# Turning the experts' input by transposing DMAs from block 2 on, with actor and router as fp16 passes over its halves

## The chip, the cores and the metric

The kernel runs on one core of a Trainium2 chip. The metric is device time in microseconds (us) of one execution; the median of the runs shown stands for a kernel.

## The reference, cut to what matters

64 batches of 128 tokens with 128 features. Each token is normalised, attends to the 120 context tokens of its batch (queries, keys and values from `Wq`, `Wk`, `Wv`), and the result is added. Then comes a mixture of experts over the normalised sum `h`:

```
probs  = softmax(h @ router_w.T)                       # 8 experts
a_h    = gelu(h @ actor_w1.T + actor_b1)               # 50 units
k      = argmax(clip(a_h @ actor_w2.T + actor_b2)) + 1 # 1 to 6
scores = where(rank(probs) < k, probs, 0)
out    = sum over e of scores[e] * ((silu(h @ gate[e].T) * (h @ up[e].T)) @ down[e].T)
result = x + out
```

All eight experts are computed for every token; a score of zero drops one. Each expert has 336 hidden units.

## The kernel before, in words

A block is four batches, so 512 tokens, and there are 16 blocks. The 8 x 336 hidden units are cut into 21 tiles of 128 rows (16 units of each expert). For a tile and a block there are three products of 128 x 128 by 128 x 512: `gate`, `up` and `down`. Each is made from fp16 halves in three passes, weights high by input low, weights low by input high, high by high (`split_product`, L408 to L412), so a tile costs TensorE nine fp16 matmuls of 512 columns. The weights are scaled by powers of two, found in the first turn, and cut into halves there (`weight_tops`, `weight_top`, `weight_scales`, `weight_low`).

Each engine runs its own program in an order written out by hand. A turn `t` has 21 steps `j`. In step `j` TensorE does the gate of tile `j + 2`, the up of tile `j` and the down of tile `j - 3` of block `t`. Between these, at a fixed `j`, each engine does a piece of the other work: the attention of block `t + 2`, and the second normalisation's turning, actor, router and ranking of block `t + 1`. ScalarE makes the silu of a tile (`gated`) and the high half of the hidden values (`high`), GpSimd weighs the silu with the scores (`weigh`), VectorE multiplies it by `up` (`hidden`) and makes the low half (`low`). Semaphores tie the engines together. Turns 0 to 3 and 12 to 16 are written out, turns 4 to 11 are a loop on the chip.

The experts' input of block `t + 1` is made as follows. ScalarE normalises it at the end of the turn before (`norm2`, tokens by partition). TensorE turns it at `j = 1` by four fp32 transposes (`turn_x2`, L362), ScalarE copies it from PSUM (`turned_x2`, L581) and casts the high half (`x2_high`, L586), GpSimd makes the low half (`x2_low`, L794). At `j = 3` `actor_router` (L369) multiplies the turned fp32 input by 64 columns of actor and router weights, twice: even 128-token groups into partitions 0 to 63, odd ones into 64 to 127. `actor`, `square` (ScalarE), `actor_arg` (VectorE), `tanh` (ScalarE), `actor_gelu` (VectorE) and `logits` (TensorE, `j = 8`) follow.

The scores of a block, spread over the 128 rows of a tile as two fp16 halves, are turned by two transposing DMAs (`turn_scores`, L278) at the end of the turn. They, the loads of x and ctx and the stores are all issued by the sync engine, in program order. `stats_1`, `aggregate_1` (VectorE) and `rstd_1` (GpSimd) begin the first normalisation of block `t + 3` from x; `turn_x` (L312), `turned_x` and `energies` (L324) carry on that of block `t + 2`.

Of the kernel before, what the change touches and what calls it, by code (L numbers as in the profile page):

```python
# [8 lines left out]
F16 = mybir.dt.float16  # L9
# [5 lines left out]
P = 128  # L15
# [37 lines left out]
W_TOP = (2.0 ** 8, 2.0 ** 15, 2.0 ** 15)  # L53
# [14 lines left out]
def program(nc, x, ctx_t, consts, consts16, gate_t, up_t, down_t, out):  # L68
# [4 lines left out]
    with ExitStack() as stack:  # L73
# [42 lines left out]
        w_max = sb("w_max", [P, 3])  # L116
        w_top_col, w_one, w_top = sb("w_top_col", [2, 2]), sb("w_one", [2, P]), sb("w_top", [2, 2 * P])
        w_half = sb("w_half", [P, 3])
        w_pow = sb("w_pow", [P, 3])
        w_inv = sb("w_inv", [P, 3])  # L120
        w_mul = sb("w_mul", [P, 3])
# [24 lines left out]
        xn_lo = [sb(f"xn_lo{k}", [P, NT], F16) for k in range(2)]  # L146

# [52 lines left out]
        hi_ready, lo_ready = sem("hi_ready"), sem("lo_ready")  # L200
        ah_done, a_ready, sq_ready, arg_ready, tanh_ready, gelu_ready, al_done, al_ready = (
# [29 lines left out]
        def upto(n):  # L231

            return min(n + 1, BLOCKS) if isinstance(n, int) else n + 1

# [15 lines left out]
        @block.sync  # L250
        def _(sp):
            def load_x(n, par):
                wait(sp, x2_ready, n - 1)
                sp.dma_start(x_in[par][:], x_blocks[n]).then_inc(x_loaded[par], 16)

            def load_ctx(n, par):
                wait(sp, vp_done, n - 1)
                sp.dma_start(ctx_in[par][:], ctx_blocks[n]).then_inc(ctx_loaded[par], 16)

            def load_weights(k, w):  # L260
                for c in range(3):
                    cols = slice(c * PART * P, (c + 1) * PART * P)
                    sp.dma_start(raw[k][:, cols], w[:, cols]).then_inc(weights_in[3 * k + c], 16)

            load_x(0, 0)
            load_ctx(0, 0)
            load_x(1, 1)
            load_ctx(1, 1)
            load_weights(0, gate_t)
            load_weights(1, up_t)  # L270
            load_weights(2, down_t)
            for n in range(2, 4):
                load_ctx(n, n % 2)
                load_x(n, n % 2)

            def turn_scores(n):
                for dst, src in ((unit_hi, spread_hi), (unit_lo, spread_lo)):
                    sp.dma_start(dst[:].rearrange("p (b n) -> p b n", b=BB), src[:], transpose=True)\  # L278
                        .then_inc(units_in, 16)

            def turn(t, par):
                if is_block(t + 4):
                    load_ctx(t + 4, par)
                if is_block(t + 1):
                    sp.wait_ge(spread_lo_ready, t + 1)
                if is_block(t + 4):
                    sp.dma_start(x_in[par][:], x_blocks[t + 4]).then_inc(x_loaded[par], 16)  # L290
                if is_block(t + 1):
                    turn_scores(t + 1)
                if is_block(t - 1):
                    sp.wait_ge(out_ready, t)
                    sp.dma_start(out_blocks[t - 1], out_sb[1 - par][:]).then_inc(stored[1 - par], 16)

            turns(sp, turn)
            for par in range(2):
                sp.wait_ge(stored[par], 16 * (BLOCKS // 2))

        @block.tensor
        def _(pe):
# [69 lines left out]

            def probs_transposes(n, dst=x1):
                pe.wait_ge(exp_done, n + 1)
                if dst is x1:
                    wait(pe, al_ready, upto(n - 1))
                if isinstance(n, int) and n < 2:
                    pe.wait_ge(kt_ready, n + 1)
                for b in range(BB):
                    last = transpose(dst[0:CTX, b * P:(b + 1) * P], probs[:, b, :], ident_sb)  # L380
                last.then_inc(pt_done, 1)
# [45 lines left out]
            def gate(t, par, j):  # L427
                n = TILES * t + j
                if isinstance(t, int) and t == 0 and j == 0:
                    pe.wait_ge(w_mul_ready, 1)  # L430
                if j == 0:
                    pe.wait_ge(hi_ready, t + 1)
                    pe.wait_ge(lo_ready, t + 1)
                if isinstance(t, int) and t == 0 and j % PART == 0:
# [29 lines left out]
            def turn(t, par):  # L464
                nxt = 1 - par
                for j in range(TILES):
                    if isinstance(t, int) and t == 0 and j == 2:
                        weights_turned(1, 2, 3)
                    if isinstance(t, int) and t == 0 and j == 4:
                        weights_spread(1, 2, 3)  # L470
# [68 lines left out]
        def _(act):  # L539
# [23 lines left out]
            def norm2(n, lo, hi):  # L563
                act.wait_ge(ln2_shift, n + 1)
                wait(act, t2_done, n)
# [21 lines left out]

            def keys(n, src=x1):
                act.wait_ge(kp_done, n + 1)
                wait(act, e_done, n)  # L590
                af(k_t[:], src[:, 0:NC], ACT.Identity, bias=key_col[:]).then_inc(kt_ready, 1)

            def actor(n):
                act.wait_ge(ah_done, n + 1)
                wait(act, gelu_ready, n)
                af(a_sb[:], x1[:, 0:2 * P], ACT.Identity, bias=b1_col).then_inc(a_ready, 1)

            def square(n):
                act.wait_ge(a_ready, n + 1)
                af(x1[:, 0:2 * P], x1[:, 0:2 * P], ACT.Square, bias=b1_root[:], scale=sq_scale[:]).then_inc(sq_ready, 1)  # L600
# [59 lines left out]
            def turn(t, par):  # L660
                nxt = 1 - par
                for j in range(TILES):
# [12 lines left out]
                    if j == 1 and is_block(t + 1):  # L675
                        turned_x2(t + 1)
                    if j == 2 and is_block(t + 1):
                        x2_high(t + 1, nxt)
                    if j == 4 and is_block(t + 1):
                        actor(t + 1)  # L680
                        square(t + 1)
# [23 lines left out]
                    if j == 20 and is_block(t + 2):  # L705
                        norm2(t + 2, 2, BB)
                    if isinstance(t, int) and t == 0 and j == 0:
                        keys(2)
# [12 lines left out]
            act.wait_ge(setup_pool, 8)  # L721
# [32 lines left out]
        def _(pool):  # L754
# [7 lines left out]
            for k in range(3):  # L762
                g.memset(w_half[:, k:k + 1], W_TOP[k] / 2).then_inc(setup_pool, 1)
            pool.wait_ge(setup_pool, 8)
# [93 lines left out]
            def turn(t, par):  # L858
                nxt = 1 - par
                for j in range(TILES):  # L860
# [5 lines left out]
                    if j == 2 and is_block(t + 3):  # L866
                        rstd_1(t + 3)
                    if j == 3 and is_block(t + 1):
# [3 lines left out]
                    if j == 11 and is_block(t + 1):  # L872
                        count_less(t + 1)
# [26 lines left out]
        def _(dve):  # L900
# [8 lines left out]
            def weight_tops(i, lo, hi):  # L909
                dve.wait_ge(w_stat, 3)  # L910
                dve.wait_ge(w_sum_ready, 3 * i + 3)
                v.tensor_reduce(w_max[:, lo:hi], w_abs[:, lo:hi, :], AX.X, ALU.max).then_inc(w_max_ready, 1)
# [9 lines left out]
            def weight_scales(i, lo, hi):  # L922
# [9 lines left out]
                if i == 0:  # L932
                    dve.wait_ge(setup_pool, 8)
# [195 lines left out]
            def turn(t, par):  # L1129
                nxt = 1 - par  # L1130
                for j in range(TILES):
                    if j == 0 and is_block(t + 3):
                        stats_1(t + 3, nxt)
                    if j == 5 and is_block(t + 1):
# [31 lines left out]
                    if isinstance(t, int) and t == 0 and j == 3:  # L1166
                        weight_top(1, 2, 3)
                    if isinstance(t, int) and t == 0 and j == 5:
                        weight_scales(1, 2, 3)
                        result_scale()  # L1170
                    if isinstance(t, int) and t == 0 and j in LOW_AT:
# [3 lines left out]
                    if j == 1 and is_block(t + 3):  # L1175
# [10 lines left out]
                    if j == 1 and is_block(t + 3):  # L1186
# [22 lines left out]
            v.memset(w_one[:], 1.0)  # L1209
            norm1(0, 0)  # L1210
# [107 lines left out]
```

## Time and profile before

| | us |
|---|---|
| median of 3 runs (801.4 to 803.35) | 802.43 |
| the profiled execution | 804.05 |
| its span, first to last instruction | 802.2 |

The profile is of one execution. Busy time of TensorE overlaps itself, because matmuls are pipelined and their ends are modelled: what a matmul costs the stream is the distance from its start to the next one's. Lines such as L362 are those of the kernel before.

### The profile page before, as it was taken

How to read it: one execution, taken by the hardware profiler on the slowest of the kernel's cores; microseconds unless marked ns; L12 is line 12 of the kernel's file. 1: busy time of each engine (PE TensorE's matmuls, PEld its weight loads, DVE VectorE, ACT ScalarE, POOL GpSimd, SP SyncE). 2: the span in 40 equal slices, each digit the busy share in tenths (PEclk: the TensorE clock that was granted, in tenths of full speed). 3: DMA queues.
4: the chain of work that ended last, by engine and by line, in shares of the span. 5: the costliest groups of instructions: out<-in, count | busy, mean ns of one | idle time of the engine just before them, and what ended most of it. 6: DMA issues, size and time to landing. Idle time of an engine off the chain costs nothing.

```text
span 802.2 us, 13994 instructions
## 1 busy us (share of the span) xinstructions
PE 773.1 (96%) x3848; PEld 391.4 (49%) x3848; DVE 627.1 (78%) x1351; ACT 591.0 (74%) x1032; POOL 553.8 (69%) x621
## 2 busy tenths in 40 slices
PE   7578999999999999999999999999999999999997
PEld 4333455454545545454554545555454555544443
DVE  4898878787787868868786887878688786877775
ACT  3577777877786777777777777777778778677654
POOL 2375776868587685858768586776858677686763
PEclk9699999999999999999999999999999999999999
DMA  7100101001010010101001010100101000010100
GB/s 293 40 1 13 27 2 32 21 13 40 14 40 2 14 40 13 39 12 39 0 12 39 12 39 12 39 0 12 39 12 41 0 23 6 1 27 0 28 1 27
DMA packets 37151, 21.41 MB, mean 27 GB/s; under 512 B 17264, under 2 KB 35824, under 8 KB 37104
## 3 DMA queue, kind: packets, MB, share of 16 engines
q1 hardware_dynamic: 36816, 20.39, 9.0%
q10 hardware_dynamic: 288, 0.48, 0.2%
q8 instruction: 19, 0.31, 0.2%
q14 instruction: 28, 0.23, 0.1%
HBM read 12.73 MB, written 4.19 MB: 21 GB/s over the span
## 4 chain that ended last, share of the span: by engine, by line
PE 91%; DVE 4%; issue 2%; POOL 1%; ACT 1%; DMA 1%; DVEq 0%; POOLq 0%; ACTq 0%
PE bank L410 26%; PE bank L412 26%; PE bank L411 26%; PE bank L341 2%; PE bank L406 2%; PE bank L333 2%; PE bank L324 2%; PE bank L369 1%; PE bank L395 1%; PE bank L362 1%; PE bank L312 1%; DVE bank L1120 1%; PE bank L380 1%; PE bank L386 1%; DVE hid_lo L1126 1%
## 5 line engine op out<-in xcount | busy, mean ns | idle before, releaser
L855 POOL TENSOR_TENSOR weighted<-silu,score_bc 128x512 f32<-128x512 f32 x336 | 427.0, 1277 | 183.6 <-ACT silu L657 175.6
L1120 DVE SCALAR_TENSOR_TENSOR bank<-bank,h_scale,weighted 128x512 f32<-128x512 f32 x336 | 253.1, 753 | 133.8 <-PE bank L412 110.1
L651 ACT ACTIVATE hid_hi<-bank 128x512 f16<-128x512 f32 x336 | 200.4, 596 | 155.4 <-DVE bank L1120 154.3
L657 ACT ACTIVATE silu<-bank,silu_scale 128x512 f32<-128x512 f32 x336 | 230.4, 686 | 27.7 <-PE bank L412 26.5
L1126 DVE TENSOR_TENSOR hid_lo<-bank,hid_hi 128x512 f16<-128x512 f32 x336 | 228.1, 679 | 10.7 <-ACT hid_hi L651 10.6
L410 PE MATMUL bank<-xn_lo,gate_hi 128*128 128x512 f16 x336 | 128.0, 381 | 4.9 <-DVE gate_lo L947 4.9
L410 PE MATMUL bank<-hid_lo,down_hi 128*128 128x512 f16 x336 | 127.9, 381 | 0.6 <-DVE hid_lo L1126 0.6
L410 PE MATMUL bank<-xn_lo,up_hi 128*128 128x512 f16 x336 | 127.4, 379 | 0.8 <-DVE hid_lo L1126 0.7
L411 PE MATMUL bank<-hid_hi,down_lo 128*128 128x512 f16 x336 | 127.9, 381 | 0.0
L412 PE MATMUL bank<-hid_hi,down_hi 128*128 128x512 f16 x336 | 127.9, 381 | 0.0
L412 PE MATMUL bank<-xn_hi,gate_hi 128*128 128x512 f16 x336 | 127.8, 380 | 0.0
L411 PE MATMUL bank<-xn_hi,gate_lo 128*128 128x512 f16 x336 | 127.8, 380 | 0.0
L412 PE MATMUL bank<-xn_hi,up_hi 128*128 128x512 f16 x336 | 127.6, 380 | 0.0
L411 PE MATMUL bank<-xn_hi,up_lo 128*128 128x512 f16 x336 | 127.6, 380 | 0.0
L410 PEld LDWEIGHTS bank<-xn_lo,up_hi 128*128 128x128 f16 x336 | 32.8, 98 | 41.7 <-DVE hid_lo L1126 2.3
L410 PEld LDWEIGHTS bank<-hid_lo,down_hi 128*128 128x128 f16 x336 | 33.0, 98 | 41.3 <-DVE hid_lo L1126 1.8
L412 PEld LDWEIGHTS bank<-hid_hi,down_hi 128*128 128x128 f16 x336 | 33.0, 98 | 39.9 <-issue 0.6
L412 PEld LDWEIGHTS bank<-xn_hi,gate_hi 128*128 128x128 f16 x336 | 32.9, 98 | 40.0 <-issue 0.5
L411 PEld LDWEIGHTS bank<-hid_hi,down_lo 128*128 128x128 f16 x336 | 33.0, 98 | 39.7 <-issue 0.6
L410 PEld LDWEIGHTS bank<-xn_lo,gate_hi 128*128 128x128 f16 x336 | 34.4, 102 | 36.8 <-issue 11.7
L412 PEld LDWEIGHTS bank<-xn_hi,up_hi 128*128 128x128 f16 x336 | 32.9, 98 | 39.6
L411 PEld LDWEIGHTS bank<-xn_hi,up_lo 128*128 128x128 f16 x336 | 32.9, 98 | 39.2
(145 smaller groups left out, 840.1 us busy)
## 6 DMA issues: line engine op xcount, KB each, us to landing
x_in<-in_x SPq DMA_DIRECT2D x16, 256.0 KB, 2.7
out<-out_sb SPq DMA_DIRECT2D x16, 256.0 KB, 2.3
ctx_in<-in_ctx_t SPq DMA_DIRECT2D x16, 240.0 KB, 2.6
raw_gate<-in_gate_t SPq DMA_DIRECT2D x3, 448.0 KB, 6.3
raw_up<-in_up_t SPq DMA_DIRECT2D x3, 448.0 KB, 8.1
raw_down<-in_down_t SPq DMA_DIRECT2D x3, 448.0 KB, 9.8
consts_sb<-in_consts ACTq DMA_DIRECT2D x1, 403.0 KB, 3.6
unit_hi<-spread_hi SPq DMA_TRANSPOSE x15, 3.0
```

Of the source, the lines that this page charges most:

```text
L324: last = mm(dst[:, b * CTX:(b + 1) * CTX], xn_t[:, b * P:(b + 1) * P], k_t[:, b * CTX:(b + 1) * CTX], start=True, stop=True)
L333: last = mm(dst[0:CTX, b * P:(b + 1) * P], ctx_in[par][:, b * CTX:(b + 1) * CTX], wv_t, start=True, stop=True)
L341: last = mm(dst[:, b * P:(b + 1) * P], probs_t[:, b * P:(b + 1) * P], v_sb[:, b * P:(b + 1) * P], start=True, stop=True)
L406: mm(dst[:, 0:NC], key_t[:], ctx_in[par][:], start=True, stop=True).then_inc(kp_done, 1)
L410: mm(dst, w_hi[w][:, cols], lo, start=start, stop=False)
L411: mm(dst, w_lo[w][:, cols], hi, start=False, stop=False)
L412: return mm(dst, w_hi[w][:, cols], hi, start=False, stop=stop)
L651: af(hid_hi[j % HRING][:], up_bank[j % U_BANKS][:], ACT.Copy).then_inc(hid_hi_ready, 1)
L657: af(silu[j % RING][:], gate_bank[(par + j) % G_BANKS][:], ACT.Silu, scale=silu_scale[:])\
L855: g.tensor_tensor(weighted[j % RING][:], silu[j % RING][:], score_bc[par][:], ALU.mult)\
L1120: v.scalar_tensor_tensor(up_bank[j % U_BANKS][:], up_bank[j % U_BANKS][:], h_scale[:], weighted[j % RING][:], ALU.mult, ALU.mult).then_inc ...
L1126: v.tensor_tensor(hid_lo[j % HRING][:], up_bank[j % U_BANKS][:], hid_hi[j % HRING][:], ALU.subtract)\
```

## The change

For blocks 0 and 1 (`by_tensor`) the input is turned as before, except that the actor and router products stand at `j = 5`. For blocks 2 to 15 ScalarE casts the high half from the unturned input at `j = 0` (`token_high`), GpSimd makes the low half at `j = 1` (`token_low`), and two transposing DMAs write the turned halves into `xn_hi` and `xn_lo`. `turn_x2`, `turned_x2` and the old casts go for these blocks. Actor and router become six fp16 matmuls of 256 columns at `j = 5` over halves of weights and input; their weights get a power-of-two scale, found in the first turn beside that of `down`, and `actor` and `square` undo it.

The sync engine's order in a turn becomes: wait for the high half, store block `t - 2`, turn the high half, wait for the low half, load x of block `t + 3`, turn the low half, wait for the spread scores, load ctx of block `t + 4`, turn the two halves of the scores. The statistics of x move from `j = 0` and `1` to `4` and `5`, `rstd_1` from `2` to `6`, `actor` and `square` from `4` to `5`, `actor_arg` from `5` to `6`.

```diff
+        xn2_hi, xn2_lo = sb("xn2_hi", [P, NT], F16), sb("xn2_lo", [P, NT], F16)
+        ar_hi, ar_lo = sb("ar_hi", [P, HALF], F16), sb("ar_lo", [P, HALF], F16)
...
+        def by_tensor(n):
+            return isinstance(n, int) and n < 2
...
+            def turned(dst, src):
+                return sp.dma_start(dst[:].rearrange("p (b n) -> p b n", b=BB), src[:], transpose=True)
             def turn(t, par):
-                if is_block(t + 4):
-                    load_ctx(t + 4, par)
+                by_dma = is_block(t + 1) and not by_tensor(t + 1)
+                if by_dma:
+                    sp.wait_ge(hi_ready, t + 2)
+                elif is_block(t - 2):
+                    sp.wait_ge(out_ready, t - 1)
+                if is_block(t - 2):
+                    sp.dma_start(out_blocks[t - 2], out_sb[par][:]).then_inc(stored[par], 16)
+                if by_dma:
+                    turned(xn_hi[1 - par], xn2_hi).then_inc(halves_in[1 - par], 16)
+                    sp.wait_ge(lo_ready, t + 2)
+                if is_block(t + 3) and not (isinstance(t, int) and t == 0):
+                    sp.dma_start(x_in[1 - par][:], x_blocks[t + 3]).then_inc(x_loaded[1 - par], 16)
+                if by_dma:
+                    turned(xn_lo[1 - par], xn2_lo).then_inc(halves_in[1 - par], 16)
                 if is_block(t + 1):
                     sp.wait_ge(spread_lo_ready, t + 1)
                 if is_block(t + 4):
-                    sp.dma_start(x_in[par][:], x_blocks[t + 4]).then_inc(x_loaded[par], 16)
+                    sp.dma_start(ctx_in[par][:], ctx_blocks[t + 4]).then_inc(ctx_loaded[par], 16)
                 if is_block(t + 1):
-                    turn_scores(t + 1)
-                if is_block(t - 1):
-                    sp.wait_ge(out_ready, t)
-                    sp.dma_start(out_blocks[t - 1], out_sb[1 - par][:]).then_inc(stored[1 - par], 16)
+                    turned(unit_hi, spread_hi).then_inc(units_in, 16)
+                    turned(unit_lo, spread_lo).then_inc(units_in, 16)
...
+            def actor_router_split(n, par):
+                pe.wait_ge(halves_in[par], 16 * (n - par))
+                if isinstance(n, int) and n == 2:
+                    pe.wait_ge(ar_ready, 1)
+                wait(pe, kt_ready, upto(n + 1))
+                wait(pe, out_ready, n - 2)
+                for w, x, first, final in ((ar_hi, xn_lo, True, False), (ar_lo, xn_hi, False, False),
+                                           (ar_hi, xn_hi, False, True)):
+                    for odd in range(2):
+                        tokens = x[par][:].rearrange("p (h s n) -> p s h n", h=2, s=2)[:, odd]
+                        last = mm(x1[odd * HALF:(odd + 1) * HALF, 0:2 * P].rearrange("p (h n) -> p h n", h=2), w[:],
+                                  tokens, start=first, stop=final)
+                last.then_inc(ah_done, 1)
...
-                    if j == 1 and is_block(t + 1):
+                    if j == 1 and by_tensor(t + 1):
                         turn_x2(t + 1)
-                    if j == 3 and is_block(t + 1):
+                    if j == 5 and by_tensor(t + 1):
                         actor_router(t + 1)
+                    elif j == 5 and is_block(t + 1):
+                        actor_router_split(t + 1, nxt)
...
+            def token_high(n):
+                act.wait_ge(xn2_ready, n + 1)
+                af(xn2_hi[:], xn2_nat[:].rearrange("p b d -> p (b d)"), ACT.Copy).then_inc(hi_ready, 1)
+            def actor_high():
+                act.wait_ge(w_mul_ready, 2)
+                af(ar_hi[:], ar_t, ACT.Copy, scale=w_mul[:, 3:4]).then_inc(ar_hi_ready, 1)
...
+            def token_low(n):
+                pool.wait_ge(hi_ready, n + 1)
+                g.tensor_tensor(xn2_lo[:], xn2_nat[:].rearrange("p b d -> p (b d)"), xn2_hi[:], ALU.subtract)\
+                    .then_inc(lo_ready, 1)
...
+            def actor_scales():
+                dve.wait_ge(w_mul_ready, 2)
+                v.tensor_scalar(ar_scale[:], w_pow[:, 3:4], 2 / W_TOP[3], None, ALU.mult)
+                v.scalar_tensor_tensor(ar_root[:], w_pow[:, 3:4], 2 / W_TOP[3], sq_scale[:], ALU.mult, ALU.mult)
+            def actor_low():
+                dve.wait_ge(ar_hi_ready, 1)
+                v.scalar_tensor_tensor(ar_lo[:], ar_t, w_mul[:, 3:4], ar_hi[:], ALU.mult, ALU.subtract)\
+                    .then_inc(ar_ready, 1)
```

## Rows read from the trace of the kernel before

**Rows 1.** The page, parts 1 and 4: busy time, and the chain by engine.
```profile
PE 773.1 (96%) x3848; PEld 391.4 (49%) x3848; DVE 627.1 (78%) x1351; ACT 591.0 (74%) x1032; POOL 553.8 (69%) x621
...
PE 91%; DVE 4%; issue 2%; POOL 1%; ACT 1%; DMA 1%; DVEq 0%; POOLq 0%; ACTq 0%
```
**Rows 2.** Waits of all engines: waiting line, releaser, us in total, times, longest.
```profile
POOL weighted L855 <- ACT silu L657: 175.6, 170, 3.3
...
PE bank L410 <- DVE gate_lo L947: 4.9, 2, 2.6
```
**Rows 3.** Busy time of each engine by stretch, a steady one; PEclk is the granted clock.
```profile
core 0: us, PE busy (x) PEld busy (x) DVE busy (x) ACT busy (x) POOL busy (x), PEclk, DMA share, GB/s
98.00:145.00 47.00, 47.00 (x240) 24.06 (x239) 37.31 (x81) 36.19 (x65) 35.41 (x39) 1.00 0.09 23
```
**Rows 4.** TensorE in order of time, steps 1 to 4 of turn 6: start, us, what.
```profile
335.90 0.60 PE L362 MATMUL bank<-consts_sb,xn_nat 128*128 128x128 f32 x4
336.33 0.38 PE L410 MATMUL bank<-xn_lo,gate_hi 128*128 128x512 f16 x1
...
340.00 0.38 PE L412 MATMUL bank<-hid_hi,down_hi 128*128 128x512 f16 x1
340.31 0.65 PE L369 MATMUL bank<-xn_t,consts_sb 128*64 128x256 f32 x4
340.90 0.39 PE L410 MATMUL bank<-xn_lo,gate_hi 128*128 128x512 f16 x1
341.12 0.38 PE L411 MATMUL bank<-xn_hi,gate_lo 128*128 128x512 f16 x1
```
**Rows 5.** Line L369: records, ns minimum, median, maximum of one, first and last start.
```profile
L369 PE MATMUL bank<-xn_t,consts_sb x64: 379/430/689, 27.9 to 717.7; 128*64 128x256 f32 x64
```
**Rows 6.** ScalarE in order of time, the same turn.
```profile
334.94 0.68 ACT L657 ACTIVATE silu<-bank,silu_scale 128x512 f32<-128x512 f32 x1
...
339.84 0.63 ACT L586 ACTIVATE xn_hi<-xn_t 128x512 f16<-128x512 f32 x1
...
344.14 0.69 ACT L657 ACTIVATE silu<-bank,silu_scale 128x512 f32<-128x512 f32 x1 [0.19 <-PE bank L412]
344.72 0.47 ACT L596 ACTIVATE a_sb<-bank,consts_sb 128x256 f32<-128x256 f32 x1
345.22 0.54 ACT L600 ACTIVATE bank<-bank,b_root,sq_scale 128x256 f32<-128x256 f32 x1
...
346.79 0.69 ACT L575 ACTIVATE xn_t<-bank,ones_col 128x512 f32<-128x512 f32 x1
```
**Rows 7.** GpSimd in order of time, the same turn.
```profile
333.20 3.78 POOL L855 TENSOR_TENSOR weighted<-silu,score_bc 128x512 f32<-128x512 f32 x3 [0.24 <-POOL score_bc L845]
...
342.47 1.17 POOL L794 TENSOR_TENSOR xn_lo<-xn_t,xn_hi 128x512 f16<-128x512 f32 x1
```
**Rows 8.** The sync queue in order of time, end of that turn.
```profile
374.09 0.37 SPq L290 DMA_DIRECT2D x_in<-in_x  x1
374.52 1.20 SPq L278 DMA_TRANSPOSE unit_hi<-spread_hi  x1
```
**Rows 9.** The page, part 6: DMA issues, KB each, median us to landing.
```profile
x_in<-in_x SPq DMA_DIRECT2D x16, 256.0 KB, 2.7
...
unit_hi<-spread_hi SPq DMA_TRANSPOSE x15, 3.0
```
**Rows 10.** VectorE in order of time, turn 0.
```profile
47.65 0.14 DVE L912 TENSOR_REDUCE w_max<-w_abs 128x1 f32<-128x3 f32 x1
47.72 1.13 DVE L947 SCALAR_TENSOR_TENSOR gate_lo<-raw_gate,w_mul,gate_hi 128x896 f16<-128x896 f32 x1
...
53.32 2.04 DVE L947 SCALAR_TENSOR_TENSOR up_lo<-raw_up,w_mul,up_hi 128x896 f16<-128x896 f32 x1
```
**Rows 11.** TensorE in order of time, turn 0; in brackets the idle time before.
```profile
47.85 0.27 PE L420 MATMUL bank<-consts_sb,w_max 128*1 128x128 f32 x1 [1.85 <-DVE w_max L912]
...
76.03 0.39 PE L410 MATMUL bank<-xn_lo,gate_hi 128*128 128x512 f16 x1 [2.57 <-DVE gate_lo L947]
...
77.72 0.63 PE L410 MATMUL bank<-hid_lo,down_hi 128*128 128x512 f16 x1
```

More of the change, by code:

```diff
@@ L50 @@
 HALF, LOGITS = 64, KMAX + EXPERTS
-W_TOP = (2.0 ** 8, 2.0 ** 15, 2.0 ** 15)
+W_TOP = (2.0 ** 8, 2.0 ** 15, 2.0 ** 15, 2.0 ** 8)
 H_SCALE = 2.0 ** -7
@@ L115, in program @@
         w_abs = sb("w_abs", [P, 3, 3])
-        w_max = sb("w_max", [P, 3])
+        w_max = sb("w_max", [P, 4])
         w_top_col, w_one, w_top = sb("w_top_col", [2, 2]), sb("w_one", [2, P]), sb("w_top", [2, 2 * P])
[L118 to L121, printed above, removed]
+        w_half = sb("w_half", [P, 4])
+        w_pow = sb("w_pow", [P, 4])
+        w_inv = sb("w_inv", [P, 4])
+        w_mul = sb("w_mul", [P, 4])
         silu_scale = sb("silu_scale", [P, 1])
@@ L146, in program @@
         xn_lo = [sb(f"xn_lo{k}", [P, NT], F16) for k in range(2)]
+        xn2_hi, xn2_lo = sb("xn2_hi", [P, NT], F16), sb("xn2_lo", [P, NT], F16)
+        ar_hi, ar_lo = sb("ar_hi", [P, HALF], F16), sb("ar_lo", [P, HALF], F16)
+        ar_scale, ar_root = sb("ar_scale", [P, 1]), sb("ar_root", [P, 1])
         a_sb = sb("a_sb", [P, 2 * P])
@@ L200, in program @@
         hi_ready, lo_ready = sem("hi_ready"), sem("lo_ready")
+        ar_top_ready, ar_hi_ready, ar_ready = sem("ar_top_ready"), sem("ar_hi_ready"), sem("ar_ready")
+        halves_in = [sem(f"halves_in{k}") for k in range(2)]
         ah_done, a_ready, sq_ready, arg_ready, tanh_ready, gelu_ready, al_done, al_ready = (
@@ L274, in _ @@
                 load_x(n, n % 2)
[L276 to L279, printed above, removed]
+            def turned(dst, src):
+                return sp.dma_start(dst[:].rearrange("p (b n) -> p b n", b=BB), src[:], transpose=True)
             def turn(t, par):
-                if is_block(t + 4):
-                    load_ctx(t + 4, par)
+                by_dma = is_block(t + 1) and not by_tensor(t + 1)
[12 more added lines that the diff above has]
+                    turned(xn_lo[1 - par], xn2_lo).then_inc(halves_in[1 - par], 16)
                 if is_block(t + 1):
@@ L430, in gate @@
                     pe.wait_ge(w_mul_ready, 1)
-                if j == 0:
+                if j == 0 and by_tensor(t):
                     pe.wait_ge(hi_ready, t + 1)
                     pe.wait_ge(lo_ready, t + 1)
+                elif j == 0:
+                    pe.wait_ge(halves_in[par], 16 * (t - par))
                 if isinstance(t, int) and t == 0 and j % PART == 0:
@@ L467, in turn @@
                     if isinstance(t, int) and t == 0 and j == 2:
-                        weights_turned(1, 2, 3)
+                        weights_turned(1, 2, 4)
                     if isinstance(t, int) and t == 0 and j == 4:
-                        weights_spread(1, 2, 3)
-                    if j == 1 and is_block(t + 1):
+                        weights_spread(1, 2, 4)
+                    if j == 1 and by_tensor(t + 1):
                         turn_x2(t + 1)
-                    if j == 3 and is_block(t + 1):
+                    if j == 5 and by_tensor(t + 1):
                         actor_router(t + 1)
+                    elif j == 5 and is_block(t + 1):
+                        actor_router_split(t + 1, nxt)
                     if j == 4 and is_block(t + 2):
@@ L564, in norm2 @@
                 act.wait_ge(ln2_shift, n + 1)
-                wait(act, t2_done, n)
+                if isinstance(n, int) and n == 2:
+                    act.wait_ge(t2_done, 2)
+                else:
+                    act.wait_ge(lo_ready, n)
                 for b in range(lo, hi):
@@ L595, in actor @@
                 wait(act, gelu_ready, n)
-                af(a_sb[:], x1[:, 0:2 * P], ACT.Identity, bias=b1_col).then_inc(a_ready, 1)
+                if isinstance(n, int) and n == 2:
+                    act.wait_ge(ar_ready, 1)
+                af(a_sb[:], x1[:, 0:2 * P], ACT.Identity, bias=b1_col,
+                   scale=1.0 if by_tensor(n) else ar_scale[:]).then_inc(a_ready, 1)
             def square(n):
                 act.wait_ge(a_ready, n + 1)
-                af(x1[:, 0:2 * P], x1[:, 0:2 * P], ACT.Square, bias=b1_root[:], scale=sq_scale[:]).then_inc(sq_ready, 1)
+                af(x1[:, 0:2 * P], x1[:, 0:2 * P], ACT.Square, bias=b1_root[:],
+                   scale=sq_scale[:] if by_tensor(n) else ar_root[:]).then_inc(sq_ready, 1)
             def tanh(n):
@@ L674, in turn @@
                             gated(t + 1, nxt, j + LEAD - TILES)
-                    if j == 1 and is_block(t + 1):
+                    if j == 1 and by_tensor(t + 1):
                         turned_x2(t + 1)
-                    if j == 2 and is_block(t + 1):
+                    if j == 2 and by_tensor(t + 1):
                         x2_high(t + 1, nxt)
-                    if j == 4 and is_block(t + 1):
+                    if j == 5 and is_block(t + 1):
                         actor(t + 1)
@@ L706, in turn @@
                         norm2(t + 2, 2, BB)
+                    if j == 0 and is_block(t + 1) and not by_tensor(t + 1):
+                        token_high(t + 1)
+                    if isinstance(t, int) and t == 0 and j == 5:
+                        actor_high()
                     if isinstance(t, int) and t == 0 and j == 0:
@@ L720, in _ @@
             act.wait_ge(setup_dve, 4)
-            act.wait_ge(setup_pool, 8)
+            act.wait_ge(setup_pool, 9)
             keys(0)
@@ L761, in _ @@
             g.memset(ones_col[:], 1.0).then_inc(setup_pool, 1)
-            for k in range(3):
+            for k in range(4):
                 g.memset(w_half[:, k:k + 1], W_TOP[k] / 2).then_inc(setup_pool, 1)
-            pool.wait_ge(setup_pool, 8)
+            pool.wait_ge(setup_pool, 9)
             pool.wait_ge(consts_in, 16)
@@ L865, in turn @@
                             weigh(t + 1, nxt, 0)
-                    if j == 2 and is_block(t + 3):
+                    if j == 6 and is_block(t + 3):
                         rstd_1(t + 3)
-                    if j == 3 and is_block(t + 1):
+                    if j == 1 and is_block(t + 1) and not by_tensor(t + 1):
+                        token_low(t + 1)
+                    if j == 3 and by_tensor(t + 1):
                         x2_low(t + 1, nxt)
@@ L871, in turn @@
                         route_probs(t + 1)
-                    if j == 11 and is_block(t + 1):
                         count_less(t + 1)
@@ L911, in weight_tops @@
                 dve.wait_ge(w_sum_ready, 3 * i + 3)
+                if i == 1:
+                    dve.wait_ge(ar_top_ready, 1)
                 v.tensor_reduce(w_max[:, lo:hi], w_abs[:, lo:hi, :], AX.X, ALU.max).then_inc(w_max_ready, 1)
@@ L932, in weight_scales @@
                 if i == 0:
-                    dve.wait_ge(setup_pool, 8)
+                    dve.wait_ge(setup_pool, 9)
                     v.tensor_scalar(silu_scale[:], w_pow[:, 0:1], 2 / W_TOP[0], None, ALU.mult)
@@ L1131, in turn @@
                 for j in range(TILES):
-                    if j == 0 and is_block(t + 3):
+                    if j == 4 and is_block(t + 3):
                         stats_1(t + 3, nxt)
-                    if j == 5 and is_block(t + 1):
+                    if j == 6 and is_block(t + 1):
                         actor_arg(t + 1)
@@ L1166, in turn @@
                     if isinstance(t, int) and t == 0 and j == 3:
-                        weight_top(1, 2, 3)
+                        weight_top(1, 2, 4)
                     if isinstance(t, int) and t == 0 and j == 5:
-                        weight_scales(1, 2, 3)
+                        weight_scales(1, 2, 4)
                         result_scale()
+                        actor_scales()
+                    if isinstance(t, int) and t == 0 and j == 7:
+                        actor_low()
                     if isinstance(t, int) and t == 0 and j in LOW_AT:
@@ L1174, in turn @@
                         hidden(t, j)
-                    if j == 1 and is_block(t + 3):
+                    if j == 5 and is_block(t + 3):
                         aggregate_1_waits(t + 3)
@@ L1185, in turn @@
                             low(t - 1, TILES - 1)
-                    if j == 1 and is_block(t + 3):
+                    if j == 5 and is_block(t + 3):
                         aggregate_1(t + 3)
@@ L1209, in _ @@
             v.memset(w_one[:], 1.0)
+            v.tensor_reduce(w_max[:, 3:4], ar_t, AX.X, ALU.max, apply_absolute_value=True).then_inc(ar_top_ready, 1)
             norm1(0, 0)
```

2 lines of the change are left out of this document (added).

## The prediction

> **What bounds the kernel now.** I read the page first. TensorE is busy for 773.1 of 802.2 us and holds 91% of the chain of work that ended last, while VectorE is at 78%, ScalarE at 74% and GpSimd at 69% [rows 1]. Then the waits: the large ones are engines that wait for a product or for each other (GpSimd 175.6 us for ScalarE's silu), and TensorE's own largest is 4.9 us in two places, behind weight halves in the first turn [rows 2]. In a window of 47 us inside the steady turns TensorE is busy for all 47.00 at granted clock 1.00, the upper level [rows 3]. The reader is to see that in turns 1 to 14 the other engines follow TensorE, and that time taken out of its stream is time taken out of the kernel. So the change is priced in the pitch (start to start) of TensorE's stream, not in busy time: a 512-column fp16 product shows 0.38 us but the next starts 0.216 later (340.90 to 341.12) [rows 4], and a tile of nine takes 9 x 0.216 = 1.94 us.
>
> **Part 1, what leaves TensorE.** For blocks 2 to 15, 14 times, `turn_x2` goes: its four transposes start at 335.90, the stream resumes at 336.33, so 0.43 us [rows 4]. `actor_router` in fp32 goes: the product before it starts at 340.00, without it the next would start at 340.22, it starts at 340.90: 0.68 us. That is 0.09 of lead (340.31 less 340.22) and 0.59 to the next full product [rows 4]. Together 1.11 us a block.
>
> **Part 2, what comes onto TensorE.** `actor_router_split` is six fp16 products of 256 columns. A 512-column one has a pitch of 0.216, so 256 columns are put at 0.108. The question is whether the two 64-wide halves (`odd` 0 and 1) stream side by side. In fp32 they do: four records of 379 to 430 ns each [rows 5] stand in 0.65 us [rows 4], two and two. No row shows it for fp16, so it is bounded. Side by side with nothing exposed: 0.09 lead, three pairs at 0.108, and an exit of about 0.10 (estimate: the fp32 transposes take 0.43 / 4 = 0.108 for 128 columns, so an fp32 pass of 256 takes 0.216; two of them leave 0.16 of the 0.59, which I split into 0.05 between the passes and 0.10 behind them), 0.52 us. With that 0.05 between pairs too: 0.63. One after another: 0.09 + 6 x 0.108 + 0.10 = 0.84. I take 0.57, near the fp32 pair, which is the nearest row. The net gain is 1.11 - 0.57 = 0.54 us a block (0.59 at best, 0.27 if serial), and 14 x 0.54 = 7.6 us (8.3 to 3.8). The gate's two waits at tile 0 become one, the router's waits stand beside products in flight; at nothing, like those of `turn_x2`, which opened with no gap before it.
>
> **Part 3, the new path of the halves.** Tile 1 opens at 335.90 [rows 4], so tile 0 opens at 333.96; all times here count from it. ScalarE's silu of tile 2 starts at 0.98 and ends 1.66 [rows 6]; `token_high` takes the place behind it and costs what `x2_high` does, 0.63 [rows 6]: high half at 2.3. GpSimd ends its three weighted products at 333.20 + 3.78, which is 3.0 [rows 7]; `token_low`, the same shape as the 1.17 us `x2_low` [rows 7], ends at 4.2. The sync queue then issues the store (0.37, as x of the same size) and the high transpose (1.2) by 4.0, then x at 4.2 and the low transpose at 4.6 [rows 8]. Behind its two new waits stand the store, which nobody needs for two turns, x, and ctx. The order x then transpose is the one that exists now at the end of a turn: there the transpose lands 3.0 us after its issue and x 2.7 [rows 9]. So x lands at 6.9 and the low half at 7.6. The router now opens tile 5, at 5 x 1.94 + 0.43 (`turn_x`, same shape as `turn_x2`) = 10.1. Slack 2.5 us: cost nothing; gate 0 of the next turn, at tile 19, is far behind. The statistics of x stand on VectorE at tile 4, after `hidden` of tile 3 (its product is done at 3 x 1.94 + 1.3 = 7.1) and a `low`: about 8.4, slack 1.5. Queued behind either wait would be VectorE's `low`, and for that TensorE's up and down; that is what it costs if the cover goes.
>
> **Part 4, the moved steps.** ScalarE loses two copies and gains one, so it loses 0.6 us a block, off the path. But tile 5 now holds actor, square and `turned_x` together. Gate 7 is done at about 10.1 + 0.57 + 0.65 + 0.16 = 11.5; silu, actor, square start to start 0.58, 0.50 and 0.51, then `turned_x` 0.69 [rows 6]: 13.8. The energies open tile 7 at 10.1 + 0.57 + 3.88 = 14.6. Slack 0.8 us, nothing. What is late next: `tanh`, then `gelu` at tile 7, about as far behind TensorE as now. GpSimd's `rstd_1` moves from tile 2 to 6, VectorE's statistics from tiles 0 and 1 to 4 and 5; GpSimd idles 175.6 / 336 = 0.5 us a tile for silu alone [rows 2] and VectorE 22% [rows 1]. ctx moves from tile 10 to 16 and is read at tile 18 of the next turn; the unit transposes stay behind a transfer of like size. All at nothing.
>
> **Part 5, the first turn.** Here VectorE goes from one instruction straight to the next [rows 10] and TensorE waits for it: 1.85 us for the weight maximum, 2.57 later for the third gate part [rows 11]. Moving the statistics of x behind tile 4 ends the first wait up to 0.8 earlier, but the same work is due again before tile 8, so I take no gain. Added before tile 8 on VectorE: two one-column scales (0.14 each, as the one-column maximum [rows 10]), the low half of the actor weights (128 x 64, a fourteenth of the 1.13 us of a weight part [rows 10], put at 0.2), a second column in the chain (0.1, estimate from the same 0.14): 0.6 us. One reduction ahead of the first normalisation goes into the bounds. From below: -1.0, if the earlier maximum keeps its gain. From above +1.9: the weight part takes 2.04 once where it took 1.13 [rows 10], and the low half could meet such a moment.
> The Trainium skill, "SBUF — State Buffer", on the port pair that VectorE and GpSimd share, says that a VectorE instruction with two SBUF inputs blocks wholly behind a GpSimd one that reads SBUF. The 2.04 beside 1.13 agrees. By it the low half would wait for up to one 1.28 us weighted product, and the first turn would cost 1.9 instead of 0.6; the sum does not use it.
>
> **Sum.** -7.6 + 0.6 = -7.0 us. The profiled execution took 804.05 (span 802.2 and 1.85 around it), which would become 797.0; it is 1.6 above the median of the runs, so on the median 802.43 - 7.0 = 795.4.
>
> **Rivals.**
> A. The fp16 halves don't run side by side. For it: no row shows it, and two fp16 streams would want two columns a cycle where the fp32 pair wanted one. Against: the bytes a cycle are the same as in the fp32 pair, which did [rows 4, 5]. Gain 3.8 - 0.6 = 3.2: 799.2.
> B. The change takes nothing off: the time saved in the stream comes back as a wait on ScalarE's chain (energies wait for `turned_x`). It decides from 0.8 us on and cancels the gain at 0.8 + 0.54 = 1.3 us of extra lateness a turn; then 802.4 + 0.6, 803.0. For it: one tile with 3 us of ScalarE work against 2.5 of TensorE's. Against: TensorE waits for nobody in a steady turn [rows 3], and ScalarE loses 0.6 us a block.
> C. Slower: the transposes are late. Twice as many pass the sync queue, and the low half stands behind a store, a transpose and x. If it landed 5.5 us after its issue the router would open late; TensorE is in order, so gate, up and down queue behind it. From 6.0 us it eats the gain; at 7.5, three times the measured low one, the wait is 2.0 a block: 14 x (2.0 - 0.54) + 0.6 = 21, so 823. Against: the same sequence lands in 3.0 now, and the 16 engines are nearly empty at that moment.
> D. The first turn dominates: 1.9 instead of 0.6, or a second stretch at the lower clock level like the one from 76.9 to 80.3 that follows the 2.57 us wait (a product shows 0.63 there for 0.38 [rows 11]; half speed for 3.4 us loses 1.7). With the main gain: 797 to 798.5.
>
> **How the numbers follow.** Forecast 0.60 (793.1 to 797, worked out from 0.52 to 0.63 for the router and -1.0 to +1.0 in the first turn); A 0.12; D 0.11; B 0.08; C 0.09. The runs before spread over 2 us, so 0.2% (1.6 us) is about what can be told from no change. Faster by over it takes the forecast, D and most of A: 0.81; within it the rest of A and most of B: 0.10; slower: C: 0.09. The range starts below the forecast's best case by the spread of a run, 792, and ends where A with the dear first turn ends, 802.43 - 3.8 + 1.9 = 800.5, and one run's spread more: 801.5.
>
> **What would show it.** No `turn_x2` after block 1 and the distance between turns 46.7 instead of 47.2 us; six router records starting in pairs at tile 5, and 0.5 to 0.65 us from the last product before to the next behind; no wait of TensorE on a DMA; the low transpose landing near 3 us after issue; TensorE's waits in turn 0 summing to within 1 us of now. Wrong would be: TensorE idle before the router or the energies, a pair pitch near 0.22, or first-turn waits grown by 2 us.

## The result, and the profile after

| | before | after |
|---|---|---|
| median, runs beside each other (us) | 802.89 (4 runs) | 796.34 (4 runs) |
| the profiled execution | 804.05 | 795.03 |
| its span | 802.2 | 793.2 |

The ratio is 0.992 with a 95% interval of 0.9895 to 0.9946; on another chip it was 0.9924 (0.9904 to 0.9945). By the medians that is 6.5 us less here and 5.5 on the other chip, by the ratios 6.4 and 6.1, where 7.0 had been forecast. The interval of the first ratio reaches from 4.3 to 8.4 us.

The page of the changed kernel, parts 1 and 4, beside [rows 1]:

```profile
PE 763.5 (96%) x3820; PEld 385.1 (49%) x3820; DVE 628.5 (79%) x1355; ACT 582.5 (73%) x1019; POOL 553.5 (70%) x622
...
PE 90%; DVE 4%; issue 2%; POOL 2%; ACT 1%; DMA 1%; DVEq 0%; POOLq 0%; ACTq 0%
```

TensorE lost 9.6 us of busy time and stays as full as it was; ScalarE lost 8.5, about the 0.6 a block forecast. The next fence is the busy time of each engine in two stretches of the changed kernel, which answers to [rows 3]: TensorE still has no hole and full clock. DMA's share rose from 0.09 to 0.10 and 0.12.

```profile
98.00:145.00 47.00, 46.99 (x240) 23.80 (x239) 37.49 (x82) 36.00 (x65) 35.67 (x40) 1.00 0.10 23
145.00:193.00 48.00, 48.00 (x246) 24.31 (x244) 38.59 (x83) 36.87 (x66) 35.60 (x40) 1.00 0.12 28
```

TensorE in order of time, at step 5 of two turns that follow each other; it answers to [rows 4]:

```profile
153.69 0.38 PE L447 MATMUL bank<-hid_hi,down_hi 128*128 128x512 f16 x1
154.00 0.30 PE L404 MATMUL bank<-xn_lo,ar_hi 128*64 128x256 f16 x2
154.14 0.28 PE L404 MATMUL bank<-xn_hi,ar_lo 128*64 128x256 f16 x2
154.25 0.28 PE L404 MATMUL bank<-xn_hi,ar_hi 128*64 128x256 f16 x2
154.46 0.39 PE L445 MATMUL bank<-xn_lo,gate_hi 128*128 128x512 f16 x1
...
200.63 0.30 PE L404 MATMUL bank<-xn_lo,ar_hi 128*64 128x256 f16 x2
```

The six products stand two and two, a pair 0.14 and 0.11 behind the one before, and the next full product 0.21 behind the last. Between the last full product and the next lie 0.77 us, that is 0.55 more than a pitch of 0.216. A turn is 200.63 - 154.00 = 46.63 us long. Before, the same distance from router to router was 198.31 - 151.11 = 47.20:

```profile
151.11 0.65 PE L369 MATMUL bank<-xn_t,consts_sb 128*64 128x256 f32 x4
...
198.31 0.65 PE L369 MATMUL bank<-xn_t,consts_sb 128*64 128x256 f32 x4
```

The sync queue in the same turn, and from the DMA view the landings (KB each, median us from issue). The views leave buffer numbers out, so `xn2_hi` and `xn_hi` have one name there:

```profile
145.90 0.39 SPq L300 DMA_DIRECT2D out<-out_sb  x1
146.33 1.21 SPq L287 DMA_TRANSPOSE xn_hi<-xn_hi  x1
147.84 0.38 SPq L305 DMA_DIRECT2D x_in<-in_x  x1
148.27 1.19 SPq L287 DMA_TRANSPOSE xn_lo<-xn_lo  x1
```
```profile
x_in<-in_x SPq DMA_DIRECT2D x16, 256.0 KB, 2.9
...
xn_hi<-xn_hi SPq DMA_TRANSPOSE x14, 2.7
xn_lo<-xn_lo SPq DMA_TRANSPOSE x14, 3.0
```

The low half lands at about 148.27 + 3.0 = 151.3 and is wanted at 154.0: 2.7 us to spare.

The first turn, VectorE, GpSimd and TensorE in order of time, one fence for each:

```profile
57.01 0.14 DVE L1013 TENSOR_SCALAR ar_scale<-w_pow 128x1 f32<-128x1 f32 x1
57.07 1.09 DVE L1014 SCALAR_TENSOR_TENSOR ar_root<-w_pow,sq_scale 128x1 f32<-128x1 f32 x1
58.08 0.74 DVE L1197 SCALAR_TENSOR_TENSOR bank<-bank,h_scale,weighted 128x512 f32<-128x512 f32 x1
...
62.09 0.58 DVE L1018 SCALAR_TENSOR_TENSOR ar_lo<-consts_sb,w_mul,ar_hi 128x64 f16<-128x64 f32 x1
```
```profile
56.88 1.27 POOL L919 TENSOR_TENSOR weighted<-silu,score_bc 128x512 f32<-128x512 f32 x1 [0.83 <-ACT silu L712]
```
```profile
36.29 0.59 PE L445 MATMUL bank<-xn_lo,gate_hi 128*128 128x512 f16 x1 [2.33 <-DVE gate_lo L1024]
...
77.20 0.39 PE L445 MATMUL bank<-xn_lo,gate_hi 128*128 128x512 f16 x1 [2.57 <-DVE gate_lo L1024]
```

The first gate's first product in the kernel before, for which [rows 11] has the third part:

```profile
35.96 0.59 PE L410 MATMUL bank<-xn_lo,gate_hi 128*128 128x512 f16 x1 [2.33 <-DVE gate_lo L947]
```

A product of one column by one column (`ar_root`) took 1.09 us and ended at 58.16, when GpSimd's weighted product ended (56.88 + 1.27 = 58.15). The third gate part began 77.20 - 36.29 = 40.91 us behind the first gate's first product; before, 76.03 - 35.96 = 40.07. So the first turn grew by 0.84 us up to there.

### The profile page after: what moved, and what is told of

The parts are those of the page before. It is cut to its first block, busy times and chain, and to the rows that moved or that the text cites. A ratio compares the mean times of both kernels' runs of the same rounds, so it can differ in the third digit from the quotient of the medians.

```text
span 793.2 us, 13918 instructions
## 1 busy us (share of the span) xinstructions
PE 763.5 (96%) x3820; PEld 385.1 (49%) x3820; DVE 628.5 (79%) x1355; ACT 582.5 (73%) x1019; POOL 553.5 (70%) x622
## 4 chain that ended last, share of the span: by engine, by line
PE 90%; DVE 4%; issue 2%; POOL 2%; ACT 1%; DMA 1%; DVEq 0%; POOLq 0%; ACTq 0%
PE bank L445 26%; PE bank L447 26%; PE bank L446 26%; PE bank L362 2%; PE bank L441 2%; PE bank L354 2%; PE bank L345 2%; DVE bank L1197 1%; PE bank L430 1%; POOL weighted L919 1%; PE bank L333 1%; PE bank L415 1%; PE bank L404 1%; PE bank L421 1%; DMA x_in<-in_x 1%
```

## The experiments

The theory: the gain is time taken out of TensorE's stream, 0.571 us a block, less what the first turn grew by. The rivals: it comes from ScalarE's lost copy, or from the moved statistics and the sync engine's new order.

**The change without its transposing DMAs of the input.** Every block is turned by TensorE again, with the copy from PSUM and the two old casts. The router stays split, and the moved statistics stay. The edit is cut to its main lines; waits that follow from it are left out.

```diff
-                by_dma = is_block(t + 1) and not by_tensor(t + 1)
+                by_dma = False
...
-                    if j == 1 and by_tensor(t + 1):
+                    if j == 1 and is_block(t + 1):
                         turn_x2(t + 1)
...
-                    if j == 1 and by_tensor(t + 1):
+                    if j == 1 and is_block(t + 1):
                         turned_x2(t + 1)
```

> Only the router part of the change is done: the input of every block is turned by TensorE again (four fp32 transposes, the copy from PSUM, the two casts), no transposing DMA for it; actor and router stay six fp16 products at step 5. Theory (the gain is time taken out of TensorE's stream, 0.436 us a block for the transposes and 0.135 for the router): the 14 turns are 0.436 longer than in the changed kernel, 46.63 -> 47.07 us, total 796.3 + 6.1 = 802.4. Rival (the gain comes from the copy that ScalarE loses, or from the moved statistics and the new sync order): with the copy back the rest of the change stays, so 796 to 797 if it is the moves, 802 if it is the copy; the run with ballast tells the copy from the stream.

Measured: 802.06 us, ratio to before 0.9996 (0.9979 to 1.0013).

**The whole change with ballast.** The new path stays; TensorE turns a constant at step 1, four transposes that nobody reads, as dead weight in its stream.

```diff
+            def ballast(n):
+                wait(pe, kt_ready, upto(n + 1))
+                wait(pe, out_ready, n - 2)
+                for b in range(BB):
+                    transpose(x1[:, b * P:(b + 1) * P], ident_sb, ident_sb)
...
+                    elif j == 1 and is_block(t + 1):
+                        ballast(t + 1)
```

> The whole change stays, and TensorE gets four fp32 transposes of a constant at step 1 of every turn from block 2 on, whose result nobody reads: the stream of the kernel before, without ScalarE's copy and with the transposing DMAs. Theory (stream): 0.436 a turn, 14 times, 796.3 + 6.1 = 802.4. Rival (the gain is ScalarE's lost copy or the moves): stays at 796 to 797.

Measured: 803.14 us, ratio 0.9993 (0.998 to 1.0007). TensorE's groups of instructions in this run: the ballast, 56 transposes, and one of the three router passes, as in the changed kernel.

```profile
L390 PE MATMUL bank<-consts_sb 128*128 128x128 f32 x56 | 8.4, 273 | 0.0
...
L410 PE MATMUL bank<-xn_lo,ar_hi 128*64 128x256 f16 x28 | 4.2, 297 | 0.0
```

Both runs came out at the 802.4 of the theory to within a microsecond. The changed kernel itself was not run on that chip; the run with the other order of the router's products, further down, was, with 795.84. In the traces 11 of 14 turns are 47.06 to 47.21 us long in both, for 46.62 to 46.75 in the changed kernel, as forecast. Four transposes on TensorE give the gain back, whether or not ScalarE's copy, the old casts and the transposing DMAs are there; the moved statistics, which both runs keep, give nothing that the totals show.

The traces show the router's part too. From the first gate product of block 1 to that of block 15, which is 14 turns, they have 656.8 us before, 655.1 in both these runs and 648.7 in the changed kernel. So 6.4 us are the transposes' and 1.7 the router's, for 6.1 and 1.9 by the theory. Of the 1.7 about half goes into the first turn (40.92 us to the third gate part in both runs, for 40.07), and what is left is too little for the totals to show.

**The router at step 3.** The halves come as in the changed kernel, but are wanted two steps earlier.

```diff
-                    elif j == 5 and is_block(t + 1):
+                    elif j == 3 and is_block(t + 1) and not by_tensor(t + 1):
                         actor_router_split(t + 1, nxt)
```

> The whole change stays, but TensorE's six router products stand at step 3 from block 2 on instead of step 5. In the changed kernel the low transpose is issued at 148.27 and lands some 3.0 later, and the router opens at 154.00. At step 3 it would open 2 x 1.94 + 0.43 = 4.3 earlier, at 149.7. Theory (what the halves cost is hidden by 2.7 us of slack, and TensorE in order loses whatever is later): a wait of about 1.6 us a turn on the DMA, 14 x 1.6 = 22, so 818. Rival (the slack is larger, or the other engines' slack takes the wait in): within 2 us of 796.

Measured: 833.1 us, ratio 1.0348 (1.031 to 1.0387). The slack is real and its end is where the arithmetic put it to 0.3 us, but the price is 37 us for the 22 expected. From the waits of this run, the router's total, its count and the longest:

```profile
PE bank L404 <- DMA xn_lo<-xn_lo: 26.6, 14, 2.6
```

That is 1.9 a turn for 1.6. Most of the rest is the clock. TensorE in order of time, and the busy times and granted clock by stretch, in one of these turns:

```profile
258.01 0.30 PE L404 MATMUL bank<-xn_lo,ar_hi 128*64 128x256 f16 x2 [2.20 <-DMA xn_lo<-xn_lo]
...
259.35 0.63 PE L446 MATMUL bank<-xn_hi,up_lo 128*128 128x512 f16 x1
259.78 0.63 PE L447 MATMUL bank<-xn_hi,up_hi 128*128 128x512 f16 x1
```
```profile
250.00:258.00 8.00, 5.81 (x27) 2.48 (x26) 4.83 (x8) 5.45 (x10) 6.26 (x6) 1.00 0.41 98
258.00:263.00 5.00, 4.99 (x22) 2.55 (x23) 2.13 (x6) 1.28 (x2) 1.27 (x1) 0.66 0.02 3
```

From 1.3 us behind the wait the full products stand 0.43 apart instead of 0.216, and the granted clock of those 5 us is 0.66: most of them at 1.2 GHz, the lower of its two levels. In the 14 turns with a wait the trace has seven such stretches of 3.4 us, each costing 1.7, 12 us in all; they stand behind waits of 1.9 to 2.6 us, but four other waits of 1.9 to 2.05 have none behind them. Waits and clock make 38 us, and turns 1 to 14 of this trace are together 39 longer than the changed kernel's. The profiled execution was the slowest of the four (837.34); the median is 37 above the changed kernel's.

**The router's six products in another order**, all of the even half, then all of the odd.

```diff
-                for w, x, first, final in (...):
-                    for odd in range(2):
+                for odd in range(2):
+                    for w, x, first, final in (...):
```

> The six router products in another order: all three passes into partitions 0 to 63, then all three into 64 to 127. In the changed kernel the order alternates and each pair starts 3 to 4 ns apart, 0.544 us for all. Theory (the two column halves run side by side only when neighbours in the order are of different halves): only one of three pairs overlaps, five passes of 0.108 stand in line, 0.544 + 2 x 0.108 = 0.76, 14 x 0.216 = 3.0 us: 799.3. Rival (the engine sorts them by halves itself): 796.3, pairs again. Rival (no overlap at all in this order): six in line, 0.87, 800.9.

Measured: 795.84 us, ratio 0.9896 (0.9868 to 0.9924). My theory fell; the first rival held. TensorE in order of time shows the same three pairs:

```profile
342.07 0.31 PE L404 MATMUL bank<-xn_lo,ar_hi 128*64 128x256 f16 x2
342.20 0.28 PE L404 MATMUL bank<-xn_hi,ar_lo 128*64 128x256 f16 x2
342.31 0.28 PE L404 MATMUL bank<-xn_hi,ar_hi 128*64 128x256 f16 x2
342.53 0.39 PE L445 MATMUL bank<-xn_lo,gate_hi 128*128 128x512 f16 x1
```

The whole costs 0.551 us instead of 0.544; the two of a pair start 10 ns apart instead of 3 to 4. The two column halves overlap in either order. Whether the engine or the compiler brings the pairs together is not shown.

**The changed kernel again**, as the measure for the next two on one chip.

> The changed kernel unaltered, as the measure for the two others on this chip. Theory: 14 turns x 0.571 us less than before, 8.0, and about 1 us more in the first turn, 7 in all: 796 where before is 803.

Measured: 797.65 us (6 runs, 794.99 to 798.62), ratio 0.9924 (0.9904 to 0.9945).

**The scales late.** The actor's scales and low half leave the stretch of the first turn that TensorE waits for.

```diff
                         result_scale()
-                        actor_scales()
-                    if isinstance(t, int) and t == 0 and j == 7:
+                    if isinstance(t, int) and t == 0 and j == 18:
+                        actor_scales()
                         actor_low()
```

> The changed kernel with the actor's scales and the low half of its weights made at step 18 of the first turn instead of steps 5 and 7. In the changed kernel's trace the second scale takes 1.09 us where the one before takes 0.14, and the low half 0.58; together they move VectorE's next hidden product by 1.6. Theory (VectorE sets the first turn up to step 8, and these three instructions are in its way): the third gate part is waited for until about 1.2 us earlier (77.2 -> 76.0 from the span's start), total 795.1. Rival (VectorE would only wait for GpSimd or ScalarE instead): 77.2 and 796.3.

Measured: 795.92 us, ratio 0.9912 (0.9895 to 0.993); once more on a third chip, 795.46, ratio 0.9902 (0.9885 to 0.9918).

> The late scales once more, on the chip of the run with the products in the wait: 795.9, third gate part about 39.7 us behind the first product of the first gate, as in its first run, against 40.9 in the changed kernel.

VectorE at step 18, and TensorE at the third gate part, in the first of these runs:

```profile
92.42 0.16 DVE L1014 SCALAR_TENSOR_TENSOR ar_root<-w_pow,sq_scale 128x1 f32<-128x1 f32 x1
92.48 0.28 DVE L1018 SCALAR_TENSOR_TENSOR ar_lo<-consts_sb,w_mul,ar_hi 128x64 f16<-128x64 f32 x1
```
```profile
36.25 0.59 PE L445 MATMUL bank<-xn_lo,gate_hi 128*128 128x512 f16 x1 [2.33 <-DVE gate_lo L1024]
...
75.92 0.39 PE L445 MATMUL bank<-xn_lo,gate_hi 128*128 128x512 f16 x1 [2.57 <-DVE gate_lo L1024]
```

The same instructions take 0.16 and 0.28 us here (0.21 and 0.29 in the repeat), not 1.09 and 0.58: GpSimd's weighted product ended 0.04 us after the first of them began, and operations on 128 x 4 follow it. The gate part begins 39.67 us behind the first gate: 1.24 less than in the changed kernel, as forecast (39.88 in the repeat, whose stretch at the lower clock at the start ends 8 us later). In the totals the gain does not stand clear of the intervals.

**The statistics late too**, in the first turn, on top of the late scales; cut to the first of its moves.

```diff
-                    if j == 4 and is_block(t + 3):
+                    if j == (9 if isinstance(t, int) and t == 0 else 4) and is_block(t + 3):
                         stats_1(t + 3, nxt)
...
```

> The kernel with the late scales, and in the first turn alone the statistics of x of block 3 at steps 9 and 10 (GpSimd's part at step 10) instead of 4 to 6, where VectorE stands still for ScalarE's tables. Theory (same): another 0.8 + 0.3 us of VectorE's work leaves the stretch that TensorE waits for, third gate part at about 75, total 794.0. Rival (ScalarE's weight halves and tables set the first turn from there on): no more than the late scales give, 795.1.

Measured: 795.99 us, ratio 0.9914 (0.9895 to 0.9932); the gate part 76.26 - 36.24 = 40.02 us behind. No gain, as the rival had it. ScalarE's order there, with its two table loads, is no earlier than with the scales alone (67.58 for 67.60). But the first of these lines itself waited 2.99 us for VectorE, so that ScalarE sets the first turn from there on, the rival's reason, is not shown.

```profile
67.58 0.60 ACT L706 ACTIVATE hid_hi<-bank 128x512 f16<-128x512 f32 x1 [2.99 <-DVE bank L1197]
68.08 0.68 ACT L712 ACTIVATE silu<-bank,silu_scale 128x512 f32<-128x512 f32 x1
68.77 1.28 ACT L742 ACT_TABLE_LOAD   x1
```

**Products in the wait**, on top of the late scales.

```diff
+                if isinstance(t, int) and t == 0 and j == 2 * PART:
+                    pe.wait_ge(silu_ready, n - G_BANKS + 1)
+                    for _ in range(11):
+                        mm(gate_bank[(par + j) % G_BANKS][:], w_hi[0][:, 0:P], xn_hi[par][:], start=True, stop=True)
...
```

> The kernel with the late scales, and in the first turn, where TensorE stands 2.57 us for the third gate part, eleven 512-column products into the gate bank that is about to be overwritten (2.4 us, nobody reads them). In the run of the late scales the granted clock is at its lower level for 3.4 us right behind that wait. Theory (the lower level is what the idle stretch leaves behind, and it costs half of 3.4, 1.7 us): no lower stretch near 77, 795.9 - 1.7 = 794.2. Rival (the level there is not tied to that wait, or the products push the gate back): a lower stretch all the same, 796 or more.

Measured: 794.56 us, ratio 0.9896 (0.9878 to 0.9913), beside the repeat's 795.46 on the same chip: about 1 us, less than the 1.7 expected, and within the spread of either. Stretch 76 to 81 us, in this kernel and then in the late scales beside it:

```profile
76.00:81.00 5.00, 5.00 (x29) 2.83 (x27) 5.00 (x11) 3.31 (x7) 4.06 (x4) 1.00 0.00 0
```
```profile
76.00:81.00 5.00, 4.03 (x13) 1.63 (x14) 5.00 (x8) 3.01 (x6) 4.88 (x5) 0.73 0.00 0
```

Granted clock 1.00 for 0.73: there is no lower stretch behind the filled wait, and the turn, from its first gate product to the next turn's, is 55.66 us long for 57.52. One profile does not show that the filling did it. Of the ten profiled runs that leave the wait empty, eight have the lower stretch behind it, but the first profile of the changed kernel and that of the run without the transposing DMAs have none. The median is the lowest of all versions, though not clear of the others with late scales.

## Why the prediction was right

- **What bounds the kernel.** Right. The two runs that put four transposes back into TensorE's stream are at the time of before, with everything else of the change in one of them.
- **What leaves TensorE.** 0.436 us for the transposes (0.43 predicted) and 0.678 for the fp32 router (0.68).
- **What comes onto it.** 0.544 us for 0.57, the same in all 14 turns. Rival A, no overlap of the fp16 halves, is out: pairs start 3 to 4 ns apart. The exposed gap between passes that I had carried over from fp32 is smaller in fp16: pairs put at 0.108 follow at 0.134 and 0.109, where an fp32 pair put at 0.216 took 0.267. Net 0.571, 14 times, 8.0 us for 7.6; the 14 turns of the traces differ by 8.1.
- **The new path.** The arithmetic gave the low transpose's issue 4.6 us into the turn and 2.5 us of slack; measured 4.4 and 2.7. Rival C did not come, but step 3 shows what it would have been: its estimate of 823 left out the clock and was too low.
- **The moved steps.** At nothing, as said, in turns 1 to 14: no wait of TensorE at the energies, and the turn of 46.63 rules rival B out. In the first turn the wait there grew from 0.37 to 1.10 us.
- **The first turn.** 0.84 us for 0.6, inside the bounds, but partly by luck: two terms were wrong and partly cancel. The scales and the low half, put at 0.5, cost the 1.24 that the run with late scales gives back. The moved statistics were to gain nothing; yet with the scales out of the way the third gate part comes 0.40 earlier than before (39.67 for 40.07), and TensorE's wait for the weight maximum fell from 1.85 to 1.09. The step that was short is the price of the one-column scales: 0.14 was the price of an instruction that meets nobody, and one of the two met a GpSimd product and took 1.09. The Trainium skill, "SBUF — State Buffer", section "SBUF: two separate sides", says of the port pair that VectorE and GpSimd share that a VectorE instruction with two SBUF inputs blocks wholly behind a GpSimd one that reads SBUF and started first. The trace agrees (58.16 and 58.15), and in all six profiled runs with the scales in that place the product ended 14 to 18 ns behind GpSimd's. I had applied that rule to the low half alone, which took 0.58.
- **The sum.** -8.0 + 0.84 = -7.2, against -6.5 and -5.5 in the medians on two chips. The 0.7 and 1.7 between are no more than runs of one kernel differ by, and are not explained further. The profiled executions differ by 9.0 us, -8.1 + 0.84 - 1.7, because that of before holds a stretch at the lower clock behind its third gate part (1.7 us) and that of after does not; in its repeat on another chip the stretch was there again, and the span 795.9. So the profiles alone would have overstated the gain.

## What to carry to other kernels

Where one engine's stream has no holes, price a change by the start-to-start distances in it, gap before and after included, and then show that nothing new is late; the trace of before gave the first to 0.03 us a block here and the second to 0.2. Count the small setup instructions by whom they meet, not by their size: here a one-column product took 1.09 us, longer than the 512-column one behind it (0.74). And a wait of 2 us on TensorE can cost more than 2 us: with the router at step 3 seven of 14 were followed by 3.4 us at the lower clock, 1.7 us more each.

## What the runs showed of the hardware that was not expected

- The two 64-column halves of an fp16 product overlap as in fp32, whichever order the program names them in (0.544 and 0.551 us for six products of 256 columns).
- Waits of TensorE of 0.6 to 2.6 us, once a turn, were followed in half of the turns by 3.4 us at 1.2 GHz. In the kernel before and in seven of nine later profiles the same happened once, behind the wait of 2.57 us (2.93 in one) of the first turn. In the one profile where that wait was filled with products nobody reads, it did not.
- Not every GpSimd operation holds up a VectorE one with two SBUF inputs. In the trace of before, GpSimd's `rstd`, 128 x 4, ran from 34.09 to 35.10, and a weight part on VectorE, 128 x 896, that began at 34.69 took 1.12 us, no more than others of its kind (1.13 and 1.14). There the measurement differs from the rule cited above.
- The first 60 us of the profiled runs have a granted clock of 0.77 to 0.86, so about 17 to 28 us of them are at the lower level, and the first gate's first product starts between 35.25 and 37.22. How much of the 2 to 5 us by which most runs of one kernel differ comes from that is not shown; a gain of 1 us in the first turn was clear in the traces and not in the totals.
